# One transpose instead of four for the negated row maxima of each head pair, with the spreading to query tiles moved from ScalarE to VectorE

## What is computed

```python
def _attn(xq, xc, Wq, Wk, Wv, Wo, bo):          # 16 heads of 64
    q = (xq @ Wq).reshape(B, N, HEADS, D_HEAD)
    k = (xc @ Wk).reshape(B, S, HEADS, D_HEAD)
    v = (xc @ Wv).reshape(B, S, HEADS, D_HEAD)
    scores = jnp.einsum('bnhd,bshd->bhns', q, k) * scale
    attn = jax.nn.softmax(scores, axis=-1)
    out = jnp.einsum('bhns,bshd->bnhd', attn, v).reshape(B, N, HEADS * D_HEAD)
    return out @ Wo + bo

x = _attn(_ln(x, g1, b1), _ln(x, g1, b1), Wq1, Wk1, Wv1, Wo1, bo1) + x   # self: 512 keys
x = _attn(_ln(x, g2, b2), context, Wq2, Wk2, Wv2, Wo2, bo2) + x          # cross: 154 keys
x = _geglu_ff(_ln(x, g3, b3), Wp, bp, Wf, bf) + x
```

## Time and profile before

| | |
|---|---|
| median of 3 runs | 471.89 us (471.37 to 472.52) |
| the profiled execution | 471.55 us, of which the span of the core is 469.7 us |
| PE busy | 450.1 us, 96% of the span |
| DVE, ACT, POOL busy | 254.4, 254.9, 215.0 us (54%, 54%, 46%) |
| granted clock of TensorE | 1.0 of full speed over the whole span |

### The profile page before, as it was taken

One profiled execution on the slowest core, in us unless ns is written; L12 is line 12 of the kernel. 1 busy time (PEld: TensorE's weight loads), 2 busy tenths in 40 slices (PEclk: granted clock), 3 DMA queues, 4 the chain that ended last, 5 costly groups with the idle time before them and its releaser, 6 DMA issues.

```text
span 469.7 us, 7192 instructions
## 1 busy us (share of the span) xinstructions
PE 450.1 (96%) x2854; PEld 271.5 (58%) x2854; DVE 254.4 (54%) x478; ACT 254.9 (54%) x356; POOL 215.0 (46%) x188
## 2 busy tenths in 40 slices
PE   7988897999999999999999999999999999999896
PEld 4644463566555655655555856545575555754696
DVE  2676635666645473547645566236534546543763
ACT  3854564465667365755545446556517665337633
POOL 5586101046773776644445656754227343245010
PEclk9999999999999999999999999999999999999999
DMA  8500000000000100000001100020000000000001
GB/s 261 192 1 1 1 1 0 1 1 0 1 0 1 34 1 1 0 1 1 1 0 46 33 2 2 1 68 0 1 30 17 2 1 0 2 1 0 1 10 36
DMA packets 7984, 8.89 MB, mean 19 GB/s; under 512 B 560, under 2 KB 6128, under 8 KB 7952
## 3 DMA queue, kind: packets, MB, share of 16 engines
q1 hardware_dynamic: 7952, 8.44, 5.6%
HBM read 7.92 MB, written 0.52 MB: 18 GB/s over the span
## 4 chain that ended last, share of the span: by engine, by line
PE 84%; DVE 8%; ACT 4%; issue 2%; DMA 1%; SPq 0%; DVEq 0%
PE PV L746 17%; PE ST L717 14%; PE ST L637 11%; PE M L688 7%; PE ST L719 5%; PE M L794 5%; PE DEN L761 3%; PE M L702 3%; PE ST L653 2%; PE ST L529 2%; ACT PT L1308 2%; PE M L836 2%; DVE maxw L1509 1%; PE ST L355 1%; PE ST L677 1%
## 5 line engine op out<-in xcount | busy, mean ns | idle before, releaser
L1146 POOL TENSOR_TENSOR psums<-PT 128x1024 f32<-128x1024 f32 (+1 forms) x32 | 76.2, 2380 | 141.3 <-ACT PT L1308 141.1
L1308 ACT ACTIVATE PT<-ST 128x1024 f32<-128x1024 f32 (+1 forms) x96 | 98.1, 1025 | 38.3 <-PE ST L719 37.1
L717 PE MATMUL ST<-R 64*128 64x512 f32 (+1 forms) x576 | 105.1, 406 | 0.0
L1650 DVE TENSOR_REDUCE maxw<-M 128x1 f32<-128x512 f32 x128 | 83.6, 688 | 37.1 <-PE M L688 36.8
L746 PE MATMUL PV<-PT,V 128*64 128x512 f32 (+1 forms) x384 | 89.5, 601 | 0.0
L1150 POOL TENSOR_TENSOR psums<-psums,PT 128x1024 f32<-128x1024 f32 x32 | 76.0, 2375 | 2.5
L688 PE MATMUL M<-R 64*128 64x512 f32 (+1 forms) x256 | 71.6, 363 | 1.2 <-DVE maxw L1652 0.4
L717 PEld LDWEIGHTS ST<-R 64*128 64x128 f32 (+1 forms) x576 | 57.4, 171 | 14.7 <-ACT PT L1308 8.3
L688 PEld LDWEIGHTS M<-R 64*128 64x128 f32 x256 | 36.9, 184 | 37.4 <-issue 28.4
L746 PEld LDWEIGHTS PV<-PT,V 128*64 128x64 f32 (+1 forms) x384 | 24.7, 136 | 53.1 <-issue 52.6
L1316 ACT ACTIVATE AT<-PV 128x512 f32<-128x512 f32 x32 | 19.1, 598 | 58.6 <-PE PV L746 58.5
(11 more groups left out here) (247 smaller groups left out, 681.4 us busy)
## 6 DMA issues: line engine op xcount, KB each, us to landing
Wo<-in_wo SPq DMA_DIRECT2D x2, 512.0 KB, 6.3
xnT<-in_xT SPq DMA_DIRECT2D x2, 256.0 KB, 3.2
psums<-in_sel SPq DMA_DIRECT2D x1, 512.0 KB, 4.5
X<-in_x SPq DMA_DIRECT2D x1, 512.0 KB, 6.1
w<-in_w SPq DMA_DIRECT2D x2, 256.0 KB, 6.6
PT<-in_wq SPq DMA_DIRECT2D x1, 512.0 KB, 7.4
PT<-in_wk SPq DMA_DIRECT2D x1, 512.0 KB, 7.6
PT<-in_wv SPq DMA_DIRECT2D x1, 512.0 KB, 8.0
```

What stands on the lines that cost most here:

```text
L717: return pe.matmul(u[0:ph.KC, h, :], R[head(h), g % 3, part_k, 1, k], R[head(h), g % 3, part_q, 0, :], start=(n == 0), stop=False)
L1146: ins = pool.tensor_tensor(s, p[:, 0], p[:, 1], ALU.add)
L1308: act.activation(PT1[0:ph.KC, g % 2, c], bank(("st", g, c))[0:ph.KC, :, :], ACT.Exp, scale=HD ** -0.5).then_inc(ph.exp, 1)
L1650: ins = dve.tensor_reduce(maxw[:, g % 2, c, HD * h:HD * h + 1], m[:, :], AX, ALU.max, negate=True)
```

## The change

The negated maxima of the four query tiles and two heads go into one 128x128 square of `maxw`: head h, tile c in column 64h + 16c, instead of column 64h of the square c. `turn_pair` transposes that one square. DVE then writes `mrows`: it reads the turned square (128x128, in PSUM) once for each of the four query tiles and multiplies it by a mask from `cols`, which is one in the rows 16c and 64 + 16c for tile c and zero elsewhere, so that each tile's 128 columns of `mrows` hold only its own maxima. `onesr` now has ones in all eight rows 0, 16, 32, ..., 112; the fourth product in `scores` is otherwise as before. ACT's copy is gone. On DVE the new `maxima_rows(g+1)` stands ahead of `trailing(g+2)`. POOL builds `onesr` from a column of `cols` with one copy, behind a wait for the load of `cols`, instead of three memsets; `cols` is 37 columns wide, not 32. The first block's transposes are not touched.

```diff
@@ COL
-COL = dict(bq0=0, ..., low=30, bv0=31)
-NCOL = 32
+COL = dict(bq0=0, ..., low=30, bv0=31, tile=32, ones=36)
+NCOL = 37
@@ tensor: turn_pair
                 u = claim_half(("turn", g), mrow_set, g + 1, True)
-                for qt in range(TB):
-                    ins = pe.transpose(u[:, qt * P:(qt + 1) * P], maxw[:, g % 2, qt, :], ident[:, :])
-                ins.then_inc(t_full, 1)
+                pe.transpose(u[:, 0:P], maxw[:, g % 2, 0, :], ident[:, :]).then_inc(t_full, 1)
@@ gpsimd
-            link(pool.memset(onesr[:, :].bitcast(F32), 0.0))
-            for h in range(2):
-                link(pool.memset(onesr[HD * h:HD * h + 1, :].bitcast(F32), 1.0))
+            pool.wait_ge(ld["cols"], 16)
+            k = COL["ones"]
+            link(pool.tensor_copy(onesr[:, :], cols[:, k:k + 1].to_broadcast([P, P])))
@@ scalar
-            def maxima_rows(g):
-
-                act.wait_ge(t_full, g + 1)
-                act.activation(mrows[:, g % 2, :], half_bank(("turn", g)), ACT.Copy).then_inc(mrow_set, 1)
-                maxima_rows(0)
-                    if g + 1 < NG:
-                        maxima_rows(g + 1)
@@ vector: maxima
-                        ins = dve.tensor_reduce(maxw[:, g % 2, c, HD * h:HD * h + 1], m[:, :], AX, ALU.max, negate=True)
+                        at = HD * h + 16 * c
+                        ins = dve.tensor_reduce(maxw[:, g % 2, 0, at:at + 1], m[:, :], AX, ALU.max, negate=True)
                     else:
-                        ins = dve.tensor_reduce(maxw[:, g % 2, 2 * c:2 * c + 2, HD * h],
+                        at = HD * h + 32 * c
+                        ins = dve.tensor_reduce(maxw[:, g % 2, 0, at:at + 32:16],
@@ vector: maxima_rows, called before the loop for g = 0 and in it ahead of trailing(g + 2)
+            def maxima_rows(g):
+
+                dve.wait_ge(t_full, g + 1)
+                if g >= 2:
+                    old, o = pair(g - 2)
+                    dve.wait_ge(old.st, 2 * old.units * (o + 1))
+                dve.tensor_tensor(mrows[:, g % 2, :].rearrange("p (t n) -> p t n", t=TB),
+                                  half_bank(("turn", g))[:, 0:P].unsqueeze(1).to_broadcast([P, TB, P]),
+                                  cols[:, COL["tile"]:COL["tile"] + TB].unsqueeze(2).to_broadcast([P, TB, P]),
+                                  ALU.mult).then_inc(mrow_set, 1)
@@ host
+        cols[16 * q::HD, COL["tile"] + q] = 1
+    cols[::16, COL["ones"]] = 1
```

More of the change, by code:

```diff
@@ L35 @@
 AX = mybir.AxisListType.X
-COL = dict(bq0=0, bk0=4, nq0=8, nk0=9, ln_g=10, ln_b=11, b1=12, g1=16, c1=17, g2=18, c2=19, g3=20, c3=21, bp=22, low=30, bv0=31)
-NCOL = 32
+COL = dict(bq0=0, bk0=4, nq0=8, nk0=9, ln_g=10, ln_b=11, b1=12, g1=16, c1=17, g2=18, c2=19, g3=20, c3=21, bp=22, low=30, bv0=31, tile=32, ones=36)
+NCOL = 37
 ROW = dict(bo0=0, b20=1, bo1=2, bo2=3, bf=4)
@@ L1695, in attention @@
                         normalise0(1, c - 2)
+                maxima_rows(0)
                 for g in range(NG):
@@ L1707, in attention @@
                         normalise(g // 8 - 1, SPREADS[g][0])
+                    if g + 1 < NG:
+                        maxima_rows(g + 1)
                     if g + 2 < NG:
```

## The result

The changed kernel took 465.06 us (median of 4 runs, 463.92 to 465.73) and the kernel before, measured with it, 472.12 (4 runs, 471.37 to 472.52). The ratio is 0.985 (0.983 to 0.987). The forecast was 462.6 with a range of 459.8 to 466.6. The change is faster by 7.1 us where 9.3 were forecast.

What follows compares the result with a forecast made beforehand. PE, busy for 450.1 of 469.7 us, was taken to bound the kernel. Saving 10.6 us on turns, less 0.66, 0.2 and 0.45 lost, gave 9.3: from 471.9 to 462.6 us, range 459.8 to 466.6.

Steps and rivals of the forecast that it cites:

- Three transposes are 0.33 us: PE, each of 32 turns: dropping three of four transposes saves 0.33 us, 10.6 us in all.
- the lower bound: Turn at 250.74, next product 0.36 later: one transpose keeps 0.11, so 0.25 goes per turn, 8.0 us in all.
- The estimate of 7.8 us: PE turns: the skill's 81 ns per product would make the saving 7.8 us; the prediction preferred the trace's 0.11 us.
- The new instruction takes 0.69 us and fits: DVE, each pair: the added tensor_tensor takes 0.69 us and lies in idle time before the trailing part.
- the third rival: DVE and POOL block each other, stretching the new instruction by 1.5 us to 2.2: slower, 478 us; chance 0.05.
- Loops 17 and 25 give back their 0.33: DVE work behind the trailing part, including inverse, delays PE's third maximum product: both pairs lose their gain, 0.66 us together.
- Loop 5 loses 0.2: DVE's subtraction into xl at g = 5 already ends later than PE's start: 0.2 us of the gain lost.
- The last turn loses 0.12 beyond its gain: At g = 30 the new instruction stands behind xl; PE waits 0.42 us, losing its 0.33 and 0.1 more, 0.45 counted.
- The start costs nothing: POOL's wait for cols loses about 2 us, hidden by its 2.83 us wait for a later load; wider cols cost nothing.
- ACT's relief is worth nothing: Removing 32 ACT copies of about 0.60 us counts nothing, since PE does not wait for ACT there.
- the step in which I looked for DVE's work only behind the trailing part: Search for lost gain where DVE work follows the trailing part: g = 17, 25, 5, and g = 30 behind xl.
- The first rival: DVE late in more pairs (g = 8 to 13, 18, 19, 26, 27): ten lose 4.3 us, giving 466.9; chance 0.12.

Runs made afterwards that it cites:

- one transpose on ACT's path: Kernel before with one transpose per turn, ACT's copy writing the turned square four times, no new DVE instruction: 462.26 us, ratio 0.979.
- the run with four transposes: Changed kernel with four transposes of the same square per turn, DVE multiplying by the mask, onesr by memset: 472.26 us, ratio 1.0007.
- the new order: Changed kernel, onesr by memset, inverse moved ahead of the new DVE instruction in loops 17 and 25, that instruction ahead of xl in loop 30: 462.29 us.
- its twin with the memset: Changed kernel with onesr set to one in all rows by one memset, without the wait for cols: 465.16 us, ratio 0.984.
- the last comparison: Changed kernel measured a third time, unaltered, beside kernels with PE's tail pauses filled, against the kernel before: 463.51 us, ratio 0.982.

## Why the prediction was right, and where its sum was off

The sum was 9.3 us: 10.6 for the turns, less 0.66, 0.2 and 0.45. The trace shows 8.60 - 0.13 = 8.5 us in intervals and tail.

- **Three transposes are 0.33 us.** Right. PE's busy time in them fell by 10.5, 25 intervals gained 0.29 to 0.38, and one transpose on ACT's path gave the same in 24 of these. At the place from which the lower bound was worked out the next product came 0.36 us behind the start of the turn; now it comes 0.03 behind it (248.56 and 248.59), so 0.33 went there too, and not 0.25. The estimate of 7.8 us from the Trainium skill, TensorE: Matmul & The Clock Gate, section Back-to-back issue gap, stands against a measured 10.5: each of these fp32 transposes takes 0.11 us, not 0.081.
- **The new instruction takes 0.69 us and fits.** Right: 0.691 on average over 32 cases, and in the run with four transposes the move to DVE costs 0.1 us over all intervals. The fear of a DVE instruction stretched by POOL (the third rival) came to nothing for it: 64 cases of it, run twice a turn, lie between 677 and 693 ns.
- **Loops 17 and 25 give back their 0.33.** Right, 0.34 in the trace; and the cause was DVE's own order, as the new order showed.
- **Loop 5 loses 0.2.** Right, 0.33 - 0.13. What wasn't foreseen is that the subtraction into xl itself would change: without ACT's copy it started 0.48 us earlier behind its turn and took 2.66 us, not 2.19, so that it ended 5.33 us behind the turn, as before (5.34), and 1.11 behind PE's first product, where 1.12 was counted.

```profile
170.70 2.66 DVE L1614 TENSOR_TENSOR xl<-xnT,xh 128x512 fp32r<-128x512 f32 x1 [0.18 <-ACT xh L1272]
...
173.28 1.28 DVE L1641 TENSOR_REDUCE maxw<-M 128x1 f32<-128x512 f32 x2
```

- **The last turn loses 0.12 beyond its gain.** Right: the tail grew by 0.13, with PE's weight load waiting 0.68 us for mrows. The new instruction stands behind xl, as told from the earlier trace rows:

```profile
418.43 0.27 PE L701 MATMUL M<-ident,maxw 128*128 128x128 f32 x1
419.06 2.36 POOL L1144 TENSOR_TENSOR psums<-PT 77x1024 f32<-77x1024 f32 x1 [1.05 <-ACT PT L1301]
...
420.42 1.55 DVE L1614 TENSOR_TENSOR xl<-xnT,xh 128x512 fp32r<-128x512 f32 x1 [2.60 <-ACT xh L1272]
421.89 0.68 DVE L1654 TENSOR_TENSOR mrows<-M,cols 128x512 fp32r<-128x512 f32 x1
422.62 0.14 PEld L717 LDWEIGHTS ST<-mrows,onesr 64*77 64x77 f32 x2 [0.68 <-DVE mrows L1654]
422.62 0.46 PE L717 MATMUL ST<-mrows,onesr 64*77 64x512 f32 x2 [0.20 <-DVE mrows L1654]
```

- **The start costs nothing.** Right, as far as the runs can tell. Two show it, one with the change's start alone and one without its wait.
- **ACT's relief is worth nothing.** Wrong in kind, by 0.5 us. In the first interval three transposes alone gave nothing (-0.01) and the move alone gave 0.35; both together gave 0.38, which looks like the 0.33 that was counted, but is ACT's: for this interval the sum came out by luck. Behind loop 23 the relief gave 0.14.

What the sum missed, 0.8 us in intervals:

1. Loops 18 and 26. The interval behind each gained only 0.15 and 0.14, so 2 x 0.18 is gone. There the product behind the turn spreads `recw` (the reciprocals of the softmax's sums) over the partitions, and its weight load waits for DVE's last step of the inverse, which ends that chain on DVE:

```profile
320.76 0.75 DVE L1669 SCALAR_TENSOR_TENSOR recw<-recw,cols,work 128x512 fp32r<-128x512 f32 x1
321.50 0.27 PE L701 MATMUL M<-ident,maxw 128*128 128x128 f32 x1
321.68 0.30 PEld L781 LDWEIGHTS ST<-recw,sel 128*128 128x128 f32 x2 [0.17 <-DVE recw L1669]
321.71 0.70 PE L781 MATMUL ST<-recw,sel 128*128 128x512 f32 x2
```

   The product starts 0.21 us behind the turn; before, behind four transposes, it was 0.36, and without the wait it would be 0.03, as in loop 11. It is the step in which I looked for DVE's work only behind the trailing part; this stands ahead of it. The new instruction has no part in it, since the kernel with ACT's spreading loses the same there.
2. Loop 23, gained 0.12, so 0.2 is gone. DVE's subtraction of Wk (the trailing part of some weights), in the trace of the kernel before and of the changed one:

```profile
372.27 1.23 DVE L1629 TENSOR_TENSOR Wk<-V,Wk 128x1024 fp32r<-128x1024 f32 x1 [0.52 <-ACT Wk L1405]
```
```profile
366.25 1.59 DVE L1619 TENSOR_TENSOR Wk<-V,Wk 128x1024 fp32r<-128x1024 f32 x1
...
367.76 0.85 DVE L1644 TENSOR_REDUCE maxw<-M 128x2 f32<-128x308 f32 x2
```

   It starts 1.96 us behind its turn and not 2.45, which ACT's missing copy allows. But there POOL's addition, which runs from 364.38 to 366.75, still runs for 0.5 us, and the subtraction takes 0.36 longer; before, the addition ended at 372.31, just as the subtraction began. Of 0.49 us gained on ACT, 0.13 stays. Three other traces bear this out. With four transposes the overlap is 0.40 us and the subtraction takes 1.49 us; in the new order it takes 1.61. With the new instruction twice it starts at 367.93, when POOL's addition has just ended (367.92), and takes 1.22. Both its operands are in SBUF. The Trainium skill (SBUF — State Buffer, section Who interferes with whom) says that a DVE instruction with two inputs in SBUF contends with a GpSimd instruction that reads SBUF, and one with at most one input there does not. The trace agrees, for the two subtractions with two SBUF operands and for the new instruction with one.
3. The rest of some 0.2 us is spread: the 25 good intervals have 0.32 on average where the sum had 0.33, rounded up to 10.6 for all. It has no cause that I can name.

The rest, from 8.5 to the 7.1 of the medians, is not in the sum at all. In the profiled executions it is the start: 1.47 us, which varies from one execution to the next. In the medians a start that varies by chance would cancel; what remains is the clock in the tail. 12 of 20 executions of the changed kernel and of its twin with the memset had a mean granted clock of 0.996 or less, and took 1.8 us more on average than the other eight, whose median is 463.5. Of the kernel before it was 7 of 51; six of them, at 0.996, took no longer than their neighbours, and the seventh, at 0.993, took 474.44. In the last comparison, where the changed kernel had none in four, it gained the 8.6 us that the intervals show. That the fall costs 1.6 us is shown by the two traces that caught it; that it also cost the others their 1.8 is inferred from their times. Why the clock falls more often in the changed kernel, in a part of the tail where nothing of the code was changed, stays open. It isn't one chip against another: on one and the same chip (number 7 on record) it fell in 9 of 12 executions of the changed kernel and its twin, and later in none of 4.

The first rival (DVE late in more pairs) was right in kind only: three places more and 0.6 us, where it had ten and 4.3. Of its ten, loops 18 and 26 lost something, by work ahead of the trailing part and not behind it; 8 to 13, 19 and 27 lost nothing, and loop 23 wasn't among them. Of the 2.2 us between the 9.3 forecast and the 7.1 measured, 0.8 are in the places above; the other 1.4, the falling clock, were in neither the sum nor the rivals. That the time lay inside the range even so is owed to the width that was given to the range for other reasons, and so in part to luck.

## What to carry to other kernels

On an engine that is busy for 95% of the span, removed work is worth its share of the pitch between instructions (0.11 us for one of these transposes, not the 0.27 of its record), at each place where no other engine is late. Look for such places both ahead of and behind the point where another engine's list changes: the lists of waits name them, and an instruction run twice shows in one run those behind it (six here, but not the work ahead of it in loops 18 and 26). An instruction for an engine that must wait for another one is free if it is put into that wait; moving two steps of `inverse` into it gave back what the change had lost there, and as much again.

## What the runs showed of the hardware that I had not expected

- The start of the program varies by itself: the first turn came between 93.82 and 96.44 us in traces of kernels whose start is the same or does not matter. A product of 128x512 takes 0.85 us there for the first few us and 0.43 afterwards, while the clock row says 1.0.
- The granted clock can fall to 0.54 for some 3 us behind pauses of PE of 1.08 and 0.42 us in the tail, in one execution and not in another of the same kernel with the same pauses. It cost 1.6 us.
- A DVE instruction that reads 128 columns of PSUM four times over, with a mask read 128 times over from one column each, took the same 677 to 694 ns as one that reads 512 columns of both.
- Taking a copy off ACT made a subtraction on DVE slower: it started 0.5 us earlier, ran into an addition on POOL and took 1.59 us. Started behind the addition's end, it took 1.22.
